# The mixing stage of a fused wavelet convolution block: units of 8 rows instead of 4, a short ring of h, and taps shared out in a cycle of four

## What is computed

```python
ll, lh, hl, hh = haar_dwt(x)                      # 128 x 128 pixels, 512 channels
h = gelu(batchnorm(conv1x1(concat, w_c1, b_c1)))  # 128 channels
res = h
o = dwconv3x3(h, dw_w, dw_b)                      # nine taps for each channel
o = layernorm_chw(o, gn_g, gn_b)                  # over a whole image
o = gelu(conv1x1(o, pw1_w, pw1_b))
h = conv1x1(o, pw2_w, pw2_b) + res                # called u below
h = gelu(batchnorm(conv1x1(h, w_c2, b_c2)))
x = x + haar_idwt(h)
```

## Time and profile before

| what | us |
|---|---|
| median of three runs | 5690.55 |
| lowest, highest | 5673.53, 5690.85 |
| profiled execution, its own time | 5687.8 |
| its span | 5685.9 |
| phase_mix in it, first tap on PE | 1242.0 |
| first and last residual of phase_mix | 1392.1, 2578.0 |

### The profile page before, as it was taken

The page is one execution under the profiler, slowest core; times in us unless marked ns, Lnnn a source line. Parts: engine busy times, 40 slices in busy tenths (PEclk is TensorE's granted clock), DMA queues, the critical chain, the costliest instruction groups (busy, mean ns, idle before and its releaser), DMA issues. The chain is left out here.

```text
span 5685.9 us, 67157 instructions
## 1 busy us (share of the span) xinstructions
PE 5206.1 (92%) x18136; PEld 3152.4 (55%) x18136; DVE 4380.2 (77%) x5325; ACT 3721.4 (65%) x5012; POOL 2068.4 (36%) x1397
## 2 busy tenths in 40 slices
PE   2888888986999999996689999999999999999999
PEld 1333333332555555563256666666666766666677
DVE  8555555428999999957988888888888888888833
ACT  0333333346778777754678788787887877878744
POOL 0000000028777777730023333333333333333354
PEclk9999999998999999998899999999999999999999
DMA  9999999842333333326999999999999999999986
GB/s 368 374 372 380 369 380 378 345 143 71 108 108 112 104 108 108 108 83 226 326 381 403 393 401 398 390 402 384 398 392 384 394 384 397 399 384 395 400 292 228
DMA packets 829594, 1729.83 MB, mean 304 GB/s; under 512 B 50064, under 2 KB 587152, under 8 KB 718608
## 3 DMA queue, kind: packets, MB, share of 16 engines
q1 hardware_dynamic: 755472, 1389.81, 66.9%
q10 hardware_dynamic: 73728, 335.58, 14.4%
HBM read 1050.95 MB, written 674.23 MB: 303 GB/s over the span
## 5 line engine op out<-in xcount | busy, mean ns | idle before, releaser
L1080 POOL TENSOR_TENSOR y_lo<-y_centred_tile,y_hi 128x1024 fp32r<-128x1024 f32 x512 | 1042.3, 2057 | 1728.4 <-ACT y_centred_tile L1416 1422.9
L1295 PE MATMUL blur_psum<-y_hi,band_hi 128*128 128x512 f32 x4096 | 1129.3, 417 | 8.9 <-DVE y_tile L1173 7.4
L1278 PE MATMUL conv_psum<-u_in,w_conv 128*128 128x512 f32 x2048 | 975.3, 620 | 106.2 <-DVE pair_sums L1151 81.2
L1295 PE MATMUL blur_psum<-y_lo,band_hi 128*128 128x512 f32 x4096 | 1041.8, 396 | 6.7 <-POOL y_lo L1080 6.3
L1295 PEld LDWEIGHTS blur_psum<-y_hi,band_hi 128*128 128x128 f32 x4096 | 765.8, 188 | 278.8 <-issue 100.6
L1151 DVE TENSOR_TENSOR pair_sums<-gelu_out,conv_psum 128x512 f32<-128x512 f32 x1024 | 653.1, 683 | 308.7 <-ACT conv_psum L1386 308.6
L1295 PEld LDWEIGHTS blur_psum<-y_lo,band_hi 128*128 128x128 f32 x4096 | 769.7, 188 | 199.4 <-POOL y_lo L1080 14.8
L1173 DVE SCALAR_TENSOR_TENSOR y_tile<-blur_psum,rstd_all,y_tile 128x1024 f32<-128x1024 f32 x512 | 639.4, 1276 | 160.5 <-PE blur_psum L1295 153.1
L1386 ACT ACTIVATE gelu_out<-conv_psum,bn_shift,bn_scale 128x512 f32<-128x512 f32 x512 | 397.5, 776 | 534.1 <-PE conv_psum L1278 512.7
L1278 PEld LDWEIGHTS conv_psum<-u_in,w_conv 128*128 128x128 f32 x2048 | 399.4, 198 | 559.7 <-issue 406.2
L601 POOL TENSOR_TENSOR tap_products<-tap_products 128x512 f32<-128x512 f32 x512 | 653.5, 1276 | 42.7 <-ACT tap_products L838 6.2
(11 more groups left out here) (168 smaller groups left out, 5445.2 us busy)
## 6 DMA issues: line engine op xcount, KB each, us to landing
x_tile<-x SPq DMA_DIRECT2D x256, 1024.0 KB, 10.1
y_scratch<-x_tile ACTq DMA_DIRECT2D x256, 1024.0 KB, 8.4
y_tile<-y_scratch SPq DMA_DIRECT2D x512, 512.0 KB, 10.9
out<-y_tile SPq DMA_DIRECT2D x512, 512.0 KB, 10.4
x_stream<-x SPq DMA_DIRECT2D x192, 1024.0 KB, 11.6
x_resident<-x SPq DMA_DIRECT2D x160, 1024.0 KB, 11.0
z_scratch<-z_tile ACTq DMA_DIRECT2D x256, 256.0 KB, 7.2
z_in<-z_scratch SPq DMA_DIRECT2D x256, 256.0 KB, 3.6
```

The source lines that it names most:

```text
L1080: nc.gpsimd.tensor_tensor(y_lo[:, h, part, 2:2 + W], y_c[:, part, :], y_hi[:, h, part, 2:2 + W].bitcast(F32), ALU.subtract).then_inc(s_lo, 1)
L1278: nc.tensor.matmul(cv[s][:], w[:, s * C:(s + 1) * C], u_t[:, k % US, :], start=True, stop=True).then_inc(s_mm, 1)
L1295: ins = nc.tensor.matmul(bl[t][:, 2 * c:2 * c + 2, :], wt[:, kw, :], y[:, h, ch:ch + 2, kw:kw + W], start=(m == 0 and kw == 0), stop=(m == ...
```

## The change

phase_mix is rewritten with units of 8 rows (1024 columns, 16 an image, 128 in all). What it does:

- The depthwise part is 1024 wide on DVE, ACT and POOL; its two PSUM buffers are two banks each. PE does the taps in two halves of 512.
- The pointwise part and the gram go in halves m of 512, two a unit.
- The transposes now have one bank, and the small products of the norm use it too.
- The ring of h has 6 blocks of 8 rows. SP stores each block of h to the place in DRAM that its z came from and loads it again for the residual.
- The nine taps are shared out to PE, DVE and ACT as 4, 3, 2 and 3, 4, 2 in turn for the first 19 units, and later in a cycle of four.
- The lags are counted in units: LEAVE = 21, and LAG_TAPS = 2 for PE, DVE and ACT.

The diff, cut to its core (the loops are those of SP, then DVE, then PE):

```diff
-R2 = BANK // W2
-PE_TAPS = 2
-ACT_TAPS = 3
-LEAVE = STEPS + BEHIND
-LAG_DW = 3
-LAG_TAPS = 4
+R2 = 8
+UNIT2 = R2 * W2
+HALF = BANK
+RING = 6
+O_SLOTS = 19
+PR_SLOTS = 7
+LOADED = 3
+LEAVE = 21
+ALONE = LEAVE - 2
+LAG_TAPS = 2
+LAG_STATS = 3
+FIRST_TAPS = ((4, 3, 2), (3, 4, 2))
+STEADY_TAPS = ((1, 5, 3), (1, 4, 4), (2, 4, 3), (1, 4, 4))
+def split_of(e):
+    return FIRST_TAPS[e % 2] if e < ALONE else STEADY_TAPS[e % 4]
...
-        dw_p = [ps(f"dw_psum{i}", [128, BANK]) for i in range(2)]
-        tr_p = [ps(f"transpose_psum{i}", [128, BANK]) for i in range(2)]
-        small = ps("small2", [128, 4])
+        dw_p = [ps(f"dw_psum{i}", [128, UNIT2]) for i in range(2)]
+        tr_p = ps("transpose_psum", [128, BANK])
...
+            for p in range(ALL2 + LEAVE + 1):
+                l = p - LEAVE
+                if p + 2 < ALL2:
+                    load_z(p + 2)
+                if 0 <= p - 1 < ALL2:
+                    store_h(p - 1)
+                if 0 <= l + 2 < ALL2:
+                    load_h(l + 2)
+                if 0 <= l - 1:
+                    store_u(l - 1)
...
+            def residual(m):
+                l, half = divmod(m, 2)
+                slot = l % LOADED
+                at = slice(half * HALF, (half + 1) * HALF)
+                dve.wait_ge(s_p2, m + 1)
+                dve.wait_ge(s_hin[slot], 16 * (l // LOADED + 1))
...
+                nc.vector.scalar_tensor_tensor(u_t[:, slot, at], p2_p[:], V[:, V_PW2B:V_PW2B + 1],
+                                               h_in[:, slot, at], ALU.add, ALU.add).then_inc(s_u, 1)
+            def add_tap(e, n):
+                on_pe, on_dve, _ = split_of(e)
+                if n == 0:
+                    dve.wait_ge(s_dw, 2 * e + 2)
...
+            for p in range(LAG_TAPS, ALL2 + LEAVE + 2):
+                l, e, f = p - LEAVE, p - LAG_TAPS, p - LAG_STATS
...
+                if leaving:
+                    residual(2 * l)
+                if j == LAG_BIAS and normal:
+                    norm_fold(b - 1)
+                for n in range(min(on_dve, 2)):
+                    add_tap(e, n)
+                if 0 <= f < ALL2:
+                    statistics(f, 0)
+                if leaving:
+                    residual(2 * l + 1)
...
+                for n in range(2, on_dve):
+                    add_tap(e, n)
+                if 0 <= f < ALL2:
+                    statistics(f, 1)
+                if j == LAG_COLUMNS and normal:
+                    norm_columns(b - 1)
...
+            def taps_half(e, half):
+                if half == 0:
+                    wait_rows(pe, e)
+                    if e >= 2:
+                        pe.wait_ge(s_lk_tap, DVE_BEFORE[e - 1])
...
+                ins.then_inc(s_dw, 1)
+            def pw2_half(m):
+                pe.wait_ge(s_g1, m + 1)
+                if m >= 1:
+                    pe.wait_ge(s_u, m)
+                nc.tensor.matmul(p2_p[:], w2[:], v_t[:, m % 2, :], start=True, stop=True).then_inc(s_p2, 1)
+            def transpose_half(m):
+                pe.wait_ge(s_u, m + 1)
+                if m >= 1:
+                    pe.wait_ge(s_ut, m)
...
+            for p in range(LAG_TAPS, ALL2 + LEAVE + 2):
+                e = p - LAG_TAPS
+                for half in range(2):
+                    m = 2 * (p - LEAVE) + half
+                    if 0 <= m < 2 * ALL2:
+                        pw2_half(m)
...
+                    if 0 <= m + 1 < 2 * ALL2:
+                        pw1_half(m + 1)
...
+                    if e < ALL2:
+                        taps_half(e, half)
+                    if 0 <= m - 1 < 2 * ALL2:
+                        if j == LAG_NORM and now:
+                            pe.wait_ge(s_pow, b + 1)
+                        if j == LAG_BIAS and now:
+                            pe.wait_ge(s_b1, b)
+                        transpose_half(m - 1)
+                    if 0 <= m - 3 < 2 * ALL2:
+                        gram_half(m - 3)
```

More of the change, by code:

```diff
@@ L446, in phase_mix @@
         sem = kp["sem"]
[L447 to L450, removed]
+        ring = sb("h_ring", [128, R2 * RING + 2, W2 + 2])
+        o_buf = sb("depthwise_out", [128, O_SLOTS, UNIT2])
+        z_in = sb("z_in", [128, LOADED, UNIT2])
+        h_in = sb("h_in", [128, LOADED, UNIT2])
+        diag = sb("tap_diagonals", [128, PE_MOST, C])
         w1 = sb("pw1_weights", [128, C])
@@ L539, in _, with part @@
             sp.dma_start(K[:, 0:C], const[:, 0:C]).then_inc(s_id, 16)
-            def load(e):
-                if e >= 4:
-                    sp.wait_ge(s_h, e - 3)
+            def part(d, e):
                 b, j = divmod(e, STEPS)
[L545 to L560, removed]
+                return d[b, :, j * UNIT2:(j + 1) * UNIT2]
+            def load_z(e):
+                if e >= LOADED:
+                    sp.wait_ge(s_h, e - LOADED + 1)
+                sp.dma_start(z_in[:, e % LOADED, :], part(zv, e)).then_inc(s_z[e % LOADED], 16)
@@ new lines, in store_h, with load_h, store_u @@
+            def store_h(e):
+                sp.wait_ge(s_h, e + 1)
+                sp.dma_start(by_rows(part(zv, e)), rows_of(e)).then_inc(s_hst[e % 8], 16)
+            def load_h(l):
+                if l >= LOADED:
+                    sp.wait_ge(s_u, 2 * (l - LOADED + 1))
+                sp.wait_ge(s_hst[l % 8], 16 * (l // 8 + 1))
+                sp.dma_start(h_in[:, l % LOADED, :], part(zv, l)).then_inc(s_hin[l % LOADED], 16)
+            def store_u(l):
+                sp.wait_ge(s_u, 2 * l + 2)
+                sp.dma_start(part(uv, l), u_t[:, l % LOADED, :]).then_inc(s_ust[l % LOADED], 16)
@@ L575, in gap, with power, sum_products @@
                 at = b * (STEPS + 1) + STEPS
[L576 to L586, removed]
+                wait_place(pool, at)
+                r = 1 + at % RING * R2
+                if at % RING == 0:
+                    pool.memset(ring[:, R2 * RING + 1, :], 0.0)
+                if at % RING == RING - 1:
+                    pool.memset(ring[:, 0, :], 0.0)
+                pool.memset(ring[:, r:r + R2:R2 - 1, :], 0.0).then_inc(s_fill, 1)
+            def power(n):
+                pool.wait_ge(s_pow, n)
+                nc.gpsimd.tensor_tensor(t[:, 3:4], t[:, 2:3], neg_half[:, 0:1], ALU.pow).then_inc(s_rs, 1)
+            def sum_products(e, n):
+                first = products[:, ACT_BEFORE[e] % PR_SLOTS, :]
+                pool.wait_ge(s_pr, ACT_BEFORE[e] + n + 1)
+                if n > 1:
+                    pool.wait_ge(s_add, ADD_BEFORE[e] + n - 1)
+                nc.gpsimd.tensor_tensor(first, first, products[:, (ACT_BEFORE[e] + n) % PR_SLOTS, :],
+                                        ALU.add).then_inc(s_add, 1)
+            power(1)
+            for e in range(ALL2):
                 b, j = divmod(e, STEPS)
@@ L643, in depthwise @@
[L643 to L646, removed]
-                acc = dw_p[e % 2][:]
[L648 to L653, removed]
@@ new lines, in add_tap @@
+            def add_tap(e, n):
+                on_pe, on_dve, _ = split_of(e)
+                if n == 0:
+                    dve.wait_ge(s_dw, 2 * e + 2)
+                if n == on_dve - 1 and e >= O_SLOTS:
+                    dve.wait_ge(s_p1, 2 * (e - O_SLOTS) + 2)
+                acc = dw_p[e % 2][:]
+                to = o_buf[:, e % O_SLOTS, :] if n == on_dve - 1 else acc
+                k = on_pe + n
+                taps.link(nc.vector.scalar_tensor_tensor(by_rows(to), tap(k, e), V[:, V_DWW + k:V_DWW + k + 1],
+                                                         by_rows(acc), ALU.mult, ALU.add))
@@ L719, in _ @@
         def _(pe):
[L720 removed]
+            pe.wait_ge(s_bn1, 1 + PE_MOST)
             pe.wait_ge(s_zero, 5)
[L723 to L732 removed]
@@ L749, in transpose_step @@
-            def transpose_step(l):
-                pe.wait_ge(s_u, l + 1)
-                if l >= 2:
-                    pe.wait_ge(s_ut, l - 1)
+            def taps_half(e, half):
[3 more added lines that the diff above has]
+                        pe.wait_ge(s_lk_tap, DVE_BEFORE[e - 1])
+                count = split_of(e)[0]
+                for k in range(count):
+                    ins = nc.tensor.matmul(dw_p[e % 2][:, half * HALF:(half + 1) * HALF], diag[:, k, :],
+                                           tap(k, e, half * R2 // 2, R2 // 2),
+                                           start=(k == 0), stop=(k == count - 1))
+                ins.then_inc(s_dw, 1)
@@ L797, in gelu_first @@
             def gelu_first(e):
-                act.wait_ge(s_z[e % 4], 16 * (e // 4 + 1))
-                at = block_of(e)
-                last = freed_by(at)
-                if last is not None:
-                    act.wait_ge(s_u, last + 1)
-                rows = z_in[:, e % 4, :].rearrange("p (r c) -> p r c", c=W2)
-                if at % BLOCKS == BLOCKS - 1:
-                    nc.scalar.activation(plane[:, 0, 1:1 + W2], rows[:, R2 - 1, :], ACT.Gelu,
```

(1 more changed line is left out.)

326 lines of the change are left out of this document (164 added, 162 removed).

## The result

The changed kernel takes 6082.03 us (median of 4, 6069.57 to 6091.13) against 5690.7 for the kernel before: 1.0693 times as long, 95% interval 1.0674 to 1.0711. The profiled execution has a span of 6067.8 us. The forecast was 6035 us in a range from 5920 to 6200.

A forecast was written before the change was run, and what follows sets the result against it. PE bounds the middle stage before the change, busy 1060 of 1081 us. The terms at full clock add 251 us and PE's colder clock 96, together 347: 5687.8 + 347 = 6035 us, range 5920 to 6200.

The forecast's parts named there:

- The sum: Time to the last residual at full clock: 1367 + 1287 + 52 + 123 = 2829 us, +251; clock adds 96.
- The new wait: Steady units: DVE's tap 0 waits for PE's second half, behind pw2 and residual(2l); 11.81 us a unit against 9.53.
- The ring's length: Turn of PE and DVE in 109 steady units: four units take 47.25 us, or 11.81 us a unit.
- PE's clock: Steady units: two in three PE gaps bring 3.3 us at half clock; 0.88 us a unit, +96 us.
- Rival 1: No new cold stretches on PE in the steady units: +251, 5939 us; chance 0.12.
- rival 3: Some 7 us at half clock after every PE gap: 338 on top of 251, 6277 us; chance 0.10.
- Each image: Image ends: 7.5 us for six images and some 1 us for gram_added for seven, 52 us in all.
- The aggregate chain: Image end, at the end of DVE's step: 3.16 us, now in a ring without slack.
- First units: 19 units of taps alone: 6.05 us each, 115 us; first residual at 1367 instead of 1392.1, 25 us saved.
- The stored h: Storing and reloading h, 2 MB a unit where it was 1 MB: costs nothing, covered by the 11.8 us step.
- The end: Last 19 units without taps, two halves of 3.05 us each, plus a last statistics chain: 123 us, now 105.
- Rival 2: Steady units: engines overlap after all, POOL decides at 8.9 us a unit: -88, 5600 us; chance 0.04.

The follow-up runs named there:

- experiment 1: Changed kernel with both halves of PE's taps done first, in the unit's first half-step, before pw2 of the second half: 5687.92 us, ratio 0.9988.
- experiment 3: Changed kernel with three extra filler products of 512 columns in PE's gap before pw2 of the first half: 6033.38 us, ratio 1.0594.
- early norm: Changed kernel with norm_variance and norm_bias on DVE moved ahead of tap 0, from behind residual(2l+1): 6043.40 us, ratio 1.0618.
- experiment 4: norm_variance and norm_bias on DVE moved ahead of tap 0: changed kernel 6043.40 us; kernel of experiment 3 5944.85 us.
- filler kernel with early norm: Kernel of experiment 3 with norm_variance and norm_bias on DVE moved ahead of tap 0: 5944.85 us, ratio 1.0444.
- PE ahead: Changed kernel with PE's taps one unit ahead of DVE's, as the kernel before had them: 5691.36 us, ratio 1.0000.
- experiment 6: Store of h left out, h_in loaded only three times, from z: changed kernel 6086.06 us; kernel of experiment 1 5688.71 us.
- one tap on PE: Kernel of experiment 1 with the taps split so that every steady unit has one on PE: 5647.28 us, ratio 0.9930.

## Why the prediction was right, step by step

**The sum.** Up to the last residual of the profiled execution, the forecast was 28 us too low (2829 + 96 = 2925, measured 2953.4), and that is a balance. Measured less forecast, it is +14 us for the first residual, -13 for the ring, +21 for the clock, +16 for the images and -10 for the end. Another 6 us lie behind the last residual, and the median is 12 us above the profiled execution. The mechanism was right; that 6035 came within 47 us of 6082 owes something to terms that cancel.

**The new wait.** Right, and it is the whole loss: one edit of order takes 394 us away, where the change had added 391 (experiment 1). It was to be read in the code, by asking for each wait which instruction stands ahead of its partner in the other queue. Sums of busy time pointed the other way; at 8.2 to 9.1 us an engine every one of them was below 9.53. Experiment 1 shows what they are worth when PE and DVE no longer take turns: 9.46 in clean units, 9.86 with the image ends, not 8.9.

**The ring's length.** Forecast 11.81 us, measured 11.69 where the clock is 1.00 (experiment 3). The wide tap, taken from the tail at 1.276 us, is 1.286. POOL's add of 1024 is 2.36 us, between the two rows that I had, 2.06 and 2.55; the estimate from the Trainium skill (GPSIMD Engine Reference, section 3.1), 2.2 to 2.3, was nearer than the 2.55 that I took. It decided nothing.

**PE's clock.** The granted clock was 0.87, close to the 0.9 forecast. In clean units the cold stretches cost 1.07 us each, where I had 0.88. At 0.87 from 1500 to 2300 us, some 3.5 us of each unit run at half clock (an estimate: 0.13 x 800 / 0.5 us over 60 units); I had two thirds of 3.3, or 2.2, so the cold share was low, and less of it than I thought turned into time. Rival 1 (none) and rival 3 (3.1 us a unit) both fall. From 1500 to 2300 us PE waits 51 times for a residual for 2.85 us or more; 15 times the pw2 behind it runs slow, as at 2163.68, and 36 times it starts at or near full speed, as here, some falling back a little later:

```profile
1506.27 1.10 PE L805 MATMUL pw_psum<-gelu_out,pw_weights 128*128 128x512 f32 x2 [2.85 <-DVE u_tile L693]
```

The Trainium skill's account of matmuls that start cold after the wait of every tile (TensorE: Matmul & The Clock Gate, "HAM oscillation") fits in kind; this trace disagrees on "every", with 15 of 51.

**Each image.** This term was too small. 1459.3 us for the 109 units is 185 over 109 x 11.69, and I had 52 for the images and 96 for the clock, 148. Taking 117 (109 x 1.07) for the clock leaves about 68 for the images. The pieces of my 52 were off both ways (an image's add up to 7.66, not 7.5, which is 1 us in all):

- The waits through the one transpose bank, 3.3 x 7 = 23 (1.9 for the average, 1.4 for the bias): early norm gives back 39 us by the medians, but 18.8 in the 109 units of the traces (experiment 4). So it isn't shown that this piece was too small.
- The aggregate chain was too large. Rows 8 show it for the first image of the kernel before, 3.16 us; its later images take 1.47 (1534.05 to 1535.52), the changed kernel 1.99 in every image but the last.
- gram_added was too small, 1 us. Once in each of six images PE's first gram of the next image waits for DVE to add up the last one's, which stands behind residual(2l + 1) like the other two, so this is a third wait of their kind:

```profile
2049.16 2.06 PE L834 MATMUL gram_psum<-u_transposed 128*128 128x129 f32 x8 [3.94 <-DVE gram L750]
```

In the filler kernel with early norm the two units around it take 16.0 and 12.8 us where clean ones take 12.5 and 10.9, 5.4 us an image of the 11.0 that are left there. No run moved that call.

**First units.** Of the 25 us that I saved there 5.5 are left: from the first reduction (1235.9 before, 1230.0 after) the first residual comes after 156.2 and 150.7 us. The taps ran at PE's pace, as said (12.0 us a pair). The statistics chain, which I put at 7 us, stretches from 1349.4 to 1377.7 us: with each of its links a turn later, most of the gain went there. With taps first or PE ahead the same stretch takes 138.8 and 138.9 us, so 12 us of it were the order again.

**The stored h** costs nothing (experiment 6), also when its cover is thinner. **The end:** forecast 123, measured 113.4.

**Rival 2** (the engines overlap, POOL decides, 5600 us) didn't come about in the changed kernel, and with the turns taken out its sum still isn't reached: 5688 with this split, 5647 with one tap on PE.

## What to carry to other kernels

Before adding up busy times, follow each semaphore both ways: if A's next instruction waits for B, and B's next one stands in its queue behind something that waits for A, the two engines take turns, and a second buffer doesn't help. It costs little to cure, by the order in one queue, and such a ring has two prices, the wait itself and the clock that PE loses in it. When a stage gets a new order, count the rings through the small chains, too, such as a norm at the end of an image: each link there can cost a turn. And a price read from the first image of a stage is not that of the later ones.

## What was not expected of the hardware

Some small DVE operations stood until a POOL add was done. In the changed kernel, as the first image is folded:

```profile
1362.43 2.34 POOL L655 TENSOR_TENSOR depthwise_out<-depthwise_out,tap_products 128x1024 f32<-128x1024 f32 x1
1362.76 2.02 DVE L738 TENSOR_TENSOR small_columns<-small_columns,vectors 128x1 f32<-128x1 f32 x1
1364.73 2.34 POOL L640 TENSOR_TENSOR tap_products<-tap_products 128x1024 f32<-128x1024 f32 x1
1364.82 2.33 DVE L739 TENSOR_SCALAR pw_folded<-pw_weights,small_columns 128x128 f32<-128x128 f32 x1
1367.19 0.22 DVE L740 SCALAR_TENSOR_TENSOR small_columns<-small_columns,vectors 128x1 f32<-128x1 f32 x1
```

One column takes 2.02 us, and both end with a POOL add, to 0.1 us; the medians of L738 and L739 over the eight images are 0.16 and 0.29 us. In the next six images those two are short, and L740 stands instead, 2.19 us each time (0.22 in the first image), until the adds of POOL end:

```profile
2004.81 7.41 POOL L640 TENSOR_TENSOR tap_products<-tap_products 128x1024 f32<-128x1024 f32 x3
...
2010.04 2.20 DVE L740 SCALAR_TENSOR_TENSOR small_columns<-small_columns,vectors 128x1 f32<-128x1 f32 x1
```

The Trainium skill (GPSIMD Engine Reference, section 1) says that the two engines share their SBUF interfaces and that a DVE instruction with two SBUF inputs, or in a two-port mode, contends with POOL; the trace agrees for L738 and L740, which have two SBUF inputs, with 1.9 and 2.0 us more than alone; L739 stood, too, but whether it ran in such a mode no run shows. DVE's wide taps, which read PSUM and SBUF, keep their 1.28 us beside the same adds. Rows 8 had the same thing, 0.77 and 1.30 us an operation beside adds of 1.27, and I took the whole for DVE's own price. Wider adds on POOL make one such wait longer (2.19 us where the kernel before has 1.12 in most images), but not the chain: the fold's three operations take 2.6 us there (1539.94 to 1542.55) and 2.7 here (2009.51 to 2012.24), since two of them stand in the kernel before and one here.

The second thing is how regular the cold clock is. From the third image on, the 16 units of the changed kernel repeat to 0.02 us, cold stretches and all, 215.04 us an image.
